# A fused attention and mixture-of-experts layer: the last four chunks of its first stage written out as straight lines, the shared expert moved, and the padding rows put in front of each expert's rows

## What is computed

```python
Q, K, V = x @ Wq.T, x @ Wk.T, x @ Wv.T          # 16 heads of 16
scores = einsum('bshd,bstd->bsht', Q, K) / 4    # head against head, of one token
out = einsum('bsht,bstd->bshd', softmax(scores), V) @ Wfc.T
x = layernorm(x + out)
# experts: 32, of 128 inner units, 4 of them per token
scores = sigmoid(x @ router_weight.T)
sfc = scores + router_bias                      # 4 groups of 8; the best 2 groups are kept
topk_idx = top_k(sfc where its group is kept, 4)
topk_w = scores[topk_idx] / sum * 2.5
mixed = sum over the 4 picks of topk_w * down(silu(gate(x)) * up(x))
shared = shared_down(silu(shared_gate(x)) * shared_up(x))   # 256 inner units, all tokens
x = layernorm(x + mixed + shared)
```

## Time and profile before

| | us |
|---|---|
| median of 3 runs (lowest, highest) | 706.63 (700.69, 710.6) |
| the profiled execution, its own time | 701.5 |
| its span, first to last instruction | 699.9 |

### The profile page before, as it was taken

The page is one execution under the profiler, slowest core; times in us unless marked ns, Lnnn a source line. Parts: engine busy times, 40 slices in busy tenths (PEclk is TensorE's granted clock), DMA queues, the critical chain, the costliest instruction groups (busy, mean ns, idle before and its releaser), DMA issues.

```text
span 699.9 us, 16465 instructions
## 1 busy us (share of the span) xinstructions
PE 576.8 (82%) x4916; PEld 447.1 (64%) x4917; DVE 389.2 (56%) x1285; ACT 241.1 (34%) x490; POOL 346.3 (49%) x346
## 2 busy tenths in 40 slices
PE   6955799999999996978750099999999999993993
PEld 2541658585757666665530088988888888882872
DVE  2161538484857668557570046666666666561864
ACT  2312133425161514231230045555455554450224
POOL 4052302756565664736557326566566656562121
PEclk9978799999999999788895599999999999996997
DMA  6958492948685699377317435555555555545995
GB/s 229 239 123 224 126 216 64 270 133 242 184 225 172 188 309 340 120 258 281 145 70 242 153 109 155 155 155 164 152 149 144 164 154 165 145 136 188 419 411 219
DMA packets 124956, 135.34 MB, mean 193 GB/s; under 512 B 77288, under 2 KB 105967, under 8 KB 124272
## 3 DMA queue, kind: packets, MB, share of 16 engines
q1 hardware_dynamic: 105424, 92.95, 46.6%
q0 software_dynamic: 13248, 35.72, 13.5%
q10 hardware_dynamic: 6240, 6.09, 2.5%
HBM read 74.79 MB, written 60.96 MB: 194 GB/s over the span
## 4 chain that ended last, share of the span: by engine, by line
PE 61%; DMA 11%; DVE 8%; issue 8%; SPq 4%; ACT 3%; POOL 2%; POOLq 1%; DVEq 1%; ACTq 0%
PE bank L631 56%; PE bank L790 3%; DMA prod<-expert_rows 3%; DMA wgu_sb<-pick_rows 3%; SPq L376 1%; ACT prod L547 1%; DVE prod L1120 1%; DMA pick_rows<-prod,ids 1%; POOLq L248 1%; DMA q_slots<-wd_sb 1%; POOL expert_rows L448 1%; DVEq L241 1%; DMA k_slots<-wd_sb 1%; SPq L378 1%; PE bank L732 1%
## 5 line engine op out<-in xcount | busy, mean ns | idle before, releaser
L470 POOL DMA_INDIRECT pick_rows<-prod,ids x136 | 136.1, 1001 | 106.2 <-issue 41.1
L448 POOL DMA_INDIRECT expert_rows<-stage,pos x128 | 127.7, 998 | 62.7 <-issue 38.4
L631 PE MATMUL bank<-prod 128*128 128x128 f32 x1088 | 135.8, 278 | 1.9 <-issue 0.8
L631 PEld LDWEIGHTS bank<-prod 128*128 128x128 f32 x1088 | 127.8, 193 | 6.2 <-issue 5.2
L439 POOL TENSOR_SCALAR wgu_sb<-wgu_sb,t_mask 128x512 f32<-128x512 f32 x32 | 49.8, 1568 | 118.7 <-DVE wgu_sb L912 118.7
L631 PE MATMUL bank<-wd_sb,wqkv_sb 128*128 128x512 f32 x192 | 86.3, 606 | 8.1 <-DMA wqkv_sb<-in_wqkv 6.2
L1120 DVE COPY prod<-wgu_sb 128x512 f32 x136 | 57.2, 462 | 60.1 <-PE bank L631 33.3
L631 PE MATMUL bank<-wgu_sb 128*32 128x64 f32 x2048 | 62.7, 296 | 22.2 <-issue 13.1
L631 PEld LDWEIGHTS bank<-wgu_sb 128*32 128x32 f32 x2048 | 59.9, 137 | 29.1 <-issue 29.1
L790 PE MATMUL bank<-ident,prod 128*128 128x128 f32 x272 | 43.4, 283 | 39.5 <-DMA prod<-expert_rows 38.5
L590 ACT ACTIVATE prod<-bank,kept 128x256 f32<-128x256 f32 x136 | 57.1, 471 | 44.5 <-DMA pick_rows<-prod,ids 22.7
(11 more groups left out here) (136 smaller groups left out, 790.0 us busy)
## 6 DMA issues: line engine op xcount, KB each, us to landing
prod<-expert_rows SPq DMA_DIRECT2D x136, 132.0 KB
wgu_sb<-pick_rows SPq DMA_DIRECT2D x32, 512.0 KB, 13.8
wgu_sb<-in_wgu SPq DMA_DIRECT2D x2, 2560.0 KB
wd_sb<-in_xT SPq DMA_DIRECT2D x8, 512.0 KB, 4.1
q_slots<-wd_sb SPq DMA_DIRECT2D x16, 256.0 KB, 4.6
k_slots<-wd_sb SPq DMA_DIRECT2D x16, 256.0 KB, 3.8
wgu_sb<-q_slots SPq DMA_DIRECT2D x16, 256.0 KB, 4.2
wgu_sb<-k_slots SPq DMA_DIRECT2D x64, 64.0 KB
```

Source lines behind the costliest of these rows:

```text
L448: pool.indirect_dma_start(xs, bass.IndirectOffsetOnAxis(ap=pos[:, i, k:k + 1], axis=0), stage[:, i, k, :], None, bounds_check=XROWS - 1, o ...
L470: pool.indirect_dma_start(z, bass.IndirectOffsetOnAxis(ap=ids[par][:, j:j + 1], axis=0), y_sb[par][:, j, :], None, bounds_check=TOPK * NTO ...
L631: return pe.matmul(dst, lhsT, rhs, start=(k == 0), stop=(k == n - 1))
```

## The change

- The loop of stage one runs only over steps 0 to 7 on TensorE, VectorE, ScalarE and GpSimd. What steps 8 to 11 did, and the gates of chunk 4, is written out call by call, in a new order on each engine. In it the shared expert's parts (`gates`, `tanh_of`, `gated`, `shared_down`, `add_shared`) of chunks 4 to 7 come later than the routing of the next chunk, and chunks 6 and 7 have some of them behind the table.
- GpSimd's powers (`invert`) of chunks 5, 6 and 7 stand between the scatters, after the first tile of chunk 4 and after the first and the second tile of chunk 5; the expansion of the last chunk's weights goes to ScalarE (`expand_late`).
- To make this possible there are two buffers of `x1T_sb` and of `pos`, chunks 6 and 7 keep their normed rows in `sx`, and the gates of chunks 4 and 5, the logits and counts of some chunks use other PSUM banks.
- Counts start at 128 and not at 0, so the first 128 rows of each region are padding. Four DMAs of ScalarE (`front_pads`, 8 experts each) write them after the logits of chunk 6; `fill_padding` and its 32 DMAs go. The table's first row of an expert is its end less its whole tiles. SyncE waits for these four DMAs and the scatters. The bytes written as padding are the same as before (32 x 128 rows).
- The last 4 experts of `wd` are loaded after the gates of chunk 6, since `x1T_sb[0]` lies there.

```diff
-GB = (2, 0)
+LATE, LAST = 4, 6
+GATE_BANKS = {f: (2, 3) if f == 0 else (0, 1) for f in range(2)}
+SPARE_BANKS = {f: (7, 6) if f == 0 else (4, 5) for f in range(2)}
...
-        x1T_sb = over(prod, 5120, KC, CT)
+        x1T_sb = [over(wd_sb, 7168, KC, CT), over(prod, 5120, KC, CT)]
...
-        pos = sb("pos", [P, TPC, TOPK], U32)
+        pos = [sb(f"pos{i}", [P, TPC, TOPK], U32) for i in range(2)]
...
-            fill_padding(sp, FILL_ACT, FILL_SP, S["filled_sp"])
             for i in range(TPC):
                 sp.wait_ge(scattered[i], 16 * TOPK * CH)
 
-            sp.wait_ge(S["filled_act"], 16 * FILL_ACT)
-            sp.wait_ge(S["filled_sp"], 16 * (FILL_SP - FILL_ACT))
-            sp.wait_ge(S["filled_pool"], 16 * (NE - FILL_SP))
-            sp.wait_ge(S["pads"], 16 * QUAD)
+            sp.wait_ge(S["pads"], 16 * (QUAD + PAD_PARTS))
...
-            pool.memset(ranks_sb[:, TPC, :], 0.0).then_inc(S["consts"], 1)
+            pool.memset(ranks_sb[:, TPC, :], float(P)).then_inc(S["consts"], 1)
...
-            for s in range(CH + 4):
+            for s in range(CH):
...
+            scatter_rows(4, (0,))
+            invert(5)
...
+            def expand_late(p, hf):
+                act.wait_ge(S["pT"], 2 * p + hf + 1)
+                act.wait_ge(S["o_ready"], 2 * p - 1 + hf)
+                for t2 in range(QB):
+                    act.activation(PTx[:, hf, :, t2 * NH:(t2 + 1) * NH],
+                                   PT[:, hf, :].rearrange("p (i m) -> p i m", m=NH),
+                                   ACT.Copy, scale=t2_mask[:, t2:t2 + 1]).then_inc(S["ptx_late"], 1)
+
+            def front_pads(part):
+                n = NE // PAD_PARTS
+                act.dma_start(xs[0:NE * REGION, :].rearrange("(e r) c -> r e c", r=REGION)
+                              [0:P, part * n:(part + 1) * n, :],
+                              pad_rows[:, :].unsqueeze(1).broadcast_to([P, n, ROW])).then_inc(S["pads"], 16)
...
-            act.wait_ge(S["tab_ready"], 1)
-            fill_padding(act, 0, FILL_ACT, S["filled_act"])
+            copy_o(6)
+            stage_rows(4)
+            exponents(7)
+            tanh_of(4, 0)
+            tanh_of(4, 1)
+            expand_late(7, 0)
+            turned(5)
+            expand_late(7, 1)
+            sigmoid_parts(5)
...
+            sigmoid_parts(6)
+            for part in range(PAD_PARTS):
+                front_pads(part)
...
+            out_project(5)
+            gates(4, 0)
+            gates(4, 1)
+            turn(5)
+            router(5)
+            weigh(7)
...
             last.then_inc(S["tabT"], 1)
+            shared_down(6)
+            gates(7, 0)
+            gates(7, 1)
+            shared_down(7)
...
                 for i in range(TPC):
-                    if e:
-                        dve.wait_ge(scattered[i], 16 * TOPK * e)
+                    if e >= 2:
+                        dve.wait_ge(scattered[i], 16 * TOPK * (e - 1))
...
             dve.memset(quadf[:, :], 0.0).then_inc(S["tab_ready"], 1)
+            add_shared(6)
+            gated(7, 0)
+            gated(7, 1)
+            add_shared(7)
```

288 lines of the change are left out of this document (203 added, 85 removed).

## The result

The changed kernel takes 674.13 us (672.78 to 674.87, four runs), the kernel before 704.81 (700.69 to 710.6, four runs on the same chip): ratio 0.954, 95% interval 0.948 to 0.960. The forecast was 674, range 658 to 690. The total is right, but by luck: it is the sum of two misses that cancel, since the first load of stage two comes later than I had it, and what follows it was shorter. So the rows have to be gone through one by one.

The account below looks back on a forecast made before the run. Stage one's end was taken as bound by GpSimd's scatters, pauses and fills. Chunk 4's start 265.8, scatters 81.9, powers 3 x 1.35, waits 4.1 and 5.6 give 361.5, landed 363.8; 32.9 us saved, forecast 674 us, range 658 to 690.

Parts of the forecast that it names:

- Chunk 4: GpSimd's first scatter of chunk 4 would start at 265.8 us instead of 278.78, 13.0 earlier.
- Chunk 5: Its row numbers would release the scatters at 291.8 us, after GpSimd had waited 4.1.
- three of the prediction's own signs: Expected: waits of 3 to 6 us before chunks 5 and 6, first load by 372, padding issues under 1 us each.
- fills this with half of the weights of chunk 7: While GpSimd computes chunk 5's power, VectorE would do four weight operations, 2.7 us, then normalise by 273.4.
- Chunk 6: Its scatters would start at 320.6 us, held by counts ending at 317.8, after GpSimd had waited 5.6.
- rival E: Padding DMAs hold ScalarE, up to 47.6 us for four, giving 712 us; below 4 no cost; chance 0.03.
- Chunk 7: Row numbers ready by 334.4 us, GpSimd free only at 341.1: no wait, 6.7 us in hand.
- Sum: Last scatter ends at 361.5 us and lands at 363.8, against 396.67 before: 32.9 us earlier.
- Stage two and three: After the first load of stage two the work was held unchanged, 303 us for stage two.
- B: GpSimd never waits because TensorE keeps its high clock, both chains 3 us shorter: 664 us; chance 0.17.
- C: The shared expert's tail, 15.8 us of TensorE, outlasts its 5 us cover: 7 later, 681 us; chance 0.18.
- D: Scatters in one run each take 0.3 us more, 19 us in all: 693 us; chance 0.05.

Follow-up runs that it names:

- the three edits: Changed kernel with padding DMAs on SyncE, exponents(7) ahead of chunk 4's last stage tile, early weight loads after chunk 3's scatters land: 665.08 us.

## Why the prediction was right, and where not

- *Chunk 4*, 265.8 by the sum, is at 266.08. K, scores and counting, taken from rows of the same blocks, hold.
- *Chunk 5*, 291.8, is at 296.31. The waits before chunks 5 and 6 are over the 3 to 6 us that I had named as a sign, the first load is later than 372, and two padding issues are over 1 us each: three of the prediction's own signs that a chain was longer than I made it. The step that failed is in the chain from the power: that VectorE "fills this with half of the weights of chunk 7". Those need ScalarE's exponents, which stand behind a stage tile, which waits for a landing. The sum has no term for this landing. Its only price for one is 2.3 us, from a quiet padding DMA; at the hand-over that is right (2.45), behind 5.6 MB of weights it was over 12 (259.74 to 272.3). The gates, 1.6 us shorter than I took them, gave nothing back, since TensorE then waited 4.48 for VectorE.
- *Chunk 6*, 320.6, is at 330.35. Its row numbers were ready at 323.47: from the end of the power (302.18) 21.3, for which I had 21.8. (My own terms give 305.6 for its logits, not the 305.9 of the text.) So 3.7 of the 9.8 us are chunk 5's, and the other 6.1 are rival E's mechanism at a third of its price: I took 0.5 us for the issue of a padding DMA, 2 for four, and gave 0.45 to 11.9 as the bounds; it was 16.31 for the four, 4.1 each in the mean, though the pieces run from 0.4 to 11.47. Some 10 of the 16.31 were covered, where the text says only that "below 4 it costs nothing"; no run has a holding near 4.
- *Chunk 7* waits for nothing, as predicted, and a power between scatters costs 1.25 (1.06 and 0.19), predicted 1.35.
- *Sum*: hand-over gain 32.9 predicted, 23.4 measured; of the missing 9.5, some 6 are ScalarE's holding before chunk 6, and the rest is what chunk 6's row numbers inherit from chunk 5. With the three edits the gain is 32.7, so nothing of size is missing beside these two stalls. (The prediction's list of pauses in the kernel before leaves out the one ahead of chunk 6's scatters, 330.1 to 338.8; no term of the sum uses it.)
- *Stage two and three* I held at 303 us. They took 298.7: 4.5 back, of which 2.8 are TensorE's shorter busy time. The forecast of 673.7 stood on the median's scale, 5.1 above the profiled execution; the changed kernel's profiled execution (673.85) lies at its median (674.13), which gives the other 5 back. Those two are luck, and they, not the working, bring 674 out.
- *Rivals*: B (no waits) did not come, though the high clock was kept in chunk 4's gates (granted clock 1.00); C (the tail shows) is out, it took 18.5 us of TensorE and not 15.8, but ended at 371.4 with its last addition, and the first rows' transposes came at 377; D (every scatter 0.3 dearer) is out, the mean is 0.996 us over 128 scatters against 0.998 before.

## What to carry to other kernels

Don't take the price of one DMA's issue for that of several large ones in a row (here 1 MB each in 1056-byte rows): put them on an engine that has nothing urgent to compute, or issue them when little else moves. Here two cost 1.27 us on a queue with nothing before them and 14.57 behind three weight loads, and four cost 5.43 with quiet DMA engines and 14.7 to 16.4 behind weights. And a buffer that is freed by the landing of a transfer must be priced with what else is in the DMA queues at that moment, not with the landing time of a quiet moment; put the work that others wait for ahead of such a wait. When a total comes out right, go through the steps all the same: here two stalls, of 10 us together, lay under a forecast that met the median.

## What had not been expected of the hardware

On ScalarE the first two of four 1056 KB DMAs cost 1.3 us or less together, the third and fourth 11.47 and 3.46; the same four cost SyncE 23.60 behind weight loads, and ScalarE only 5.43 when the DMA engines had been quiet before. The landing of a scatter went from 2.45 us to over 12 with 5.6 MB of weights under way, and that of a 512 KB write from 3.9 to 16.6. After a wait of 4.48 us TensorE's transposes and router took 1.97 and 3.62 at a granted clock of 0.50, nearly double the 1.04 and 1.97 of earlier chunks, while the gates without a wait took 7.03 at 1.00 instead of 8.58 at 0.83; with the three edits the routers of chunks 6 and 7 took 1.97 and 1.95. Two chips of the same kind differed by 10 to 13% in the time of the kernel before (775.6 at best and 797.2 in the median on the one, 696.9 and 705.1 on the other).
